# A perceiver layer on one core: order of context tiles, rounded rows and outputs in the cross-attention loop

## The reference

```python
def _L0_xattn_ref(latents, context, cos, sin, ...):
    lat = layer_norm(latents, ln_lat_g, ln_lat_b)          # 16 x 64 x 256
    ctx = layer_norm(context, ln_ctx_g, ln_ctx_b)          # 16 x 1024 x 256
    q = (lat @ Wq)                                         # 16 heads of 64
    k, v = jnp.split(ctx @ Wkv, 2, axis=-1)
    k = apply_rope(k, cos, sin)
    attn = jnp.clip(einsum(q, k) * scale, -11.0, 11.0)
    attn = softmax(attn)
    return (attn @ v) @ Wo + bo
...
x = x + _L0_xattn_ref(_layernorm(x), ctx_1024, ...)
x = x + _L0_attn_ref(_layernorm(x), ...)
x = x + _L0_ffn_ref(_layernorm(x), ...)
```

## Time and profile before

| | |
|---|---|
| runs shown | 1312.22, 1312.03, 1308.29 us; median 1312.03 |
| profiled execution | 1311.06 us, of which 1309.3 are the span of the trace |
| TensorE busy | 1247.5 us, 95% |
| VectorE, ScalarE, GpSimd busy | 936.7, 708.2, 700.2 us |
| mean granted clock of TensorE | 0.989 |
| main loop (first scores to the last step's end) | 50.6 to 1029.3 us |

### The profile page before, as it was taken

The page is one execution under the profiler, slowest core; times in us unless marked ns, Lnnn a source line. Parts: engine busy times, 40 slices in busy tenths (PEclk is TensorE's granted clock), DMA queues, the critical chain, the costliest instruction groups (busy, mean ns, idle before and its releaser), DMA issues.

```text
span 1309.3 us, 40536 instructions
## 1 busy us (share of the span) xinstructions
PE 1247.5 (95%) x16508; PEld 1032.8 (79%) x16508; DVE 936.7 (72%) x1924; ACT 708.2 (54%) x1359; POOL 700.2 (53%) x611
## 2 busy tenths in 40 slices
PE   7999999999999999999999999999999999999997
PEld 3777878778787878787778777787878778799997
DVE  5797777767677777676767767776767256668886
ACT  7655655555555655555555555555643324346664
POOL 3566666666656666566666665666644113334333
PEclk9999999999999999999999999999999989999999
DMA  6344444444444444344434444344445181465662
GB/s 227 83 96 101 107 95 99 99 104 95 94 104 101 103 106 114 92 96 99 108 93 97 98 106 97 94 105 100 106 105 135 35 260 35 156 196 184 189 193 74
DMA packets 92305, 149.95 MB, mean 115 GB/s; under 512 B 28940, under 2 KB 64216, under 8 KB 91992
## 3 DMA queue, kind: packets, MB, share of 16 engines
q1 hardware_dynamic: 88040, 143.13, 42.5%
q0 software_dynamic: 4080, 4.22, 1.6%
HBM read 66.20 MB, written 14.83 MB: 62 GB/s over the span
## 4 chain that ended last, share of the span: by engine, by line
PE 76%; DMA 11%; ACT 4%; DVE 4%; issue 3%; POOL 1%; SPq 1%; POOLq 0%; ACTq 0%; DVEq 0%
PE bank L1424 27%; PE bank L1454 26%; PE bank L1410 9%; DMA out_dram<-ys,result_no 8%; PE bank L1479 3%; PE bank L1434 2%; PE bank L1589 2%; ACT ctf L725 1%; DMA ksw<-kw 1%; PE bank L1618 1%; POOL kr L573 1%; PE bank L1761 1%; PE bank L1661 1%; ACT ct L730 1%; DVE ct L1013 1%
## 5 line engine op out<-in xcount | busy, mean ns | idle before, releaser
L573 POOL TENSOR_TENSOR kr<-kr,ksw 128x1024 f32<-128x1024 f32 x128 | 309.0, 2414 | 351.4 <-DVE pr L973 263.5
L1424 PE MATMUL bank<-ct,wk_hi 128*128 128x512 f32 x1024 | 333.8, 407 | 11.9 <-DVE ct L1013 11.9
L1454 PE MATMUL bank<-p_hi,xc 128*128 128x512 f32 x1024 | 319.5, 393 | 0.0
L725 ACT ACTIVATE ctf<-bank,vecs 128x128 f32<-128x128 f32 x256 | 103.3, 453 | 299.4 <-PE bank L1434 299.4
L1424 PEld LDWEIGHTS bank<-ct,wk_hi 128*128 128x128 f32 x1024 | 184.7, 190 | 54.6 <-issue 13.5
L1454 PEld LDWEIGHTS bank<-p_hi,xc 128*128 128x128 f32 x1024 | 189.6, 188 | 40.2
L1424 PE MATMUL bank<-ct,wk_lo 128*128 128x512 f32 x512 | 202.2, 395 | 0.0
L1454 PE MATMUL bank<-p_lo,xc 128*128 128x512 f32 x512 | 200.7, 392 | 0.0
L1013 DVE TENSOR_TENSOR ct<-ctf,ct 128x256 fp32r<-128x256 f32 x128 | 58.4, 456 | 197.6 <-ACT ct L730 197.5
L1005 DVE TENSOR_TENSOR kw<-bank,stab 128x512 f32<-128x512 f32 x256 | 175.6, 686 | 15.9 <-PE bank L1424 14.8
L996 DVE TENSOR_TENSOR p_lo<-pr,p_hi 128x1024 fp32r<-128x1024 f32 x128 | 184.8, 1444 | 2.2 <-PE bank L1454 1.1
(11 more groups left out here) (215 smaller groups left out, 1740.4 us busy)
## 6 DMA issues: line engine op xcount, KB each, us to landing
ksw<-kw SPq DMA_DIRECT2D x512, 128.0 KB
raw<-in_ctx_dram SPq DMA_DIRECT2D x32, 512.0 KB, 5.2
w_two<-in_L_ffn_W_dram SPq DMA_DIRECT2D x15, 1024.0 KB
x_slots<-fill SPq DMA_DIRECT2D x128, 64.5 KB, 3.0
w_all<-in_L_ffn_W_dram SPq DMA_DIRECT2D x4, 2048.0 KB, 16.8
wo<-in_L_ffn_W_dram SPq DMA_DIRECT2D x7, 1024.0 KB, 5.1
lsum<-l_rows SPq DMA_DIRECT2D x64, 64.0 KB, 2.8
xs<-x_slots SPq DMA_DIRECT2D x23, 129.0 KB, 2.0
```

What stands on the lines that cost most here:

```text
L573: pool.tensor_tensor(kr[:, i], kr[:, i], ksw[:, i], ALU.add).then_inc(kr_done, 1)
L725: last = act.activation(ctf[:, k], psT[:, k * P:(k + 1) * P], ACT.Identity, bias=vecs[:, 3, k:k + 1], scale=vecs[:, 2, k:k + 1])
L1424: last = pe.matmul(psK[:, a * 512:(a + 1) * 512], l[:, k, w], ct[:, h % 3, r, k], start=(m == 0), stop=(m == len(parts) - 1))
L1454: last = pe.matmul(psZ[c], xc[:, slot_, l, t, cols], r[:, i, :, t], start=(f == 0 and m == 0), stop=(f == 1 and m == len(parts) - 1), skip ...
```

## The change

Four things are moved; no arithmetic changes.

- TensorE turns tile j + 9 in step j in place of j + 8, and all that prepares or follows that tile moves with it: its statistics (j + 11), shift and normalisation (j + 10), copies (j + 9). The lead-in begins at step -10, and step -3 is a call of its own before the first keys. The turn waits for `ctf` to be written and not for the rounded part.
- ScalarE writes rounded rows of tile j + 4 in place of j + 5, and POOL their low part.
- TensorE runs outputs directly behind scores, ahead of keys. ScalarE's copy L719 stands ahead of its rounding L707, VectorE's sum L979 ahead of L996. The outputs wait for `ctf` of the tile turned in the step before.
- SP loads context by pairs of tiles, 256 KB, in every even step, each pair with a semaphore of its own.

```diff
-            def context(b, f):
-                i = b % 2 * 2 + f
-                sp.dma_start(raw[:, b % 2, f * HT:(f + 1) * HT], ctx_rows(b, f)).then_inc(ctx_ld[i], 16)
+            def context(b, i):
+                tiles = slice(2 * i, 2 * i + 2)
+                sp.dma_start(raw[:, b % 2, tiles], ctx_1024[b].rearrange("(p t) d -> p t d", t=ST)[:, tiles]).then_inc(ctx_ld[i], 16)
...
-                if j >= 0 and j % 4 == 0 and j // PAIRS + 2 < B:
-                    n, f = j // PAIRS, j % PAIRS // 4
-                    done = n * ST + (f + 1) * HT
-                    sp.wait_ge(xT_ps, done)
-                    sp.wait_ge(x_lo_done, done)
-                    context(n + 2, f)
+                if j >= 0 and j % 2 == 0 and j // PAIRS + 2 < B:
+                    sp.wait_ge(xT_ps, j + 2)
+                    sp.wait_ge(x_lo_done, j + 2)
+                    context(j // PAIRS + 2, j % PAIRS // 2)
...
-                if there(j + 5):
-                    n, t = tile_at(j + 5)
-                    pool.wait_ge(x_hi_done, j + 6)
+                if there(j + 4):
+                    n, t = tile_at(j + 4)
+                    pool.wait_ge(x_hi_done, j + 5)
...
-            for j in range(-5, STEPS):
+            for j in range(-4, STEPS):
                 step(j)
...
-                if there(j):
-                    act.wait_ge(clamp_done, j + 1)
-                    wait(act, z_ps, j // 2 * 2 - 2)
-                    act.copy(step_part(p_hi, j), pr[:]).then_inc(p_hi_done, 1)
-                if there(j + 5):
-                    n, t = tile_at(j + 5)
-                    act.wait_ge(xhat_done, j + 6)
-                    if t == 0 and j + 5 >= 3 * HT:
-                        h = (j + 5) // HT - 3
-                        act.wait_ge(z_ps, h // 2 * PAIRS + h % 2 * 2 + 6)
-                    act.copy(xc[:, n, 0, t, 0:D - 1], raw[:, (j + 5) // ST % 2, (j + 5) % ST, 0:D - 1]).then_inc(x_hi_done, 1)
                 if due(j, 7):
                     n = (j - 7) // 4
                     act.wait_ge(o_ps, n + 1)
                     wait(act, o_done, n)
                     act.copy(o_part[:], psO[1]).then_inc(o_half, 1)
-                if there(j + 8):
+                if there(j):
+                    act.wait_ge(clamp_done, j + 1)
+                    wait(act, z_ps, j // 2 * 2 - 2)
+                    act.copy(step_part(p_hi, j), pr[:]).then_inc(p_hi_done, 1)
+                if there(j + 4):
+                    n, t = tile_at(j + 4)
+                    act.wait_ge(xhat_done, j + 5)
+                    if t == 0 and j + 4 >= 3 * HT:
+                        h = (j + 4) // HT - 3
+                        act.wait_ge(z_ps, h // 2 * PAIRS + h % 2 * 2 + 6)
+                    act.copy(xc[:, n, 0, t, 0:D - 1], raw[:, (j + 4) // ST % 2, (j + 4) % ST, 0:D - 1]).then_inc(x_hi_done, 1)
+                if there(j + 9):
...
                 if g >= 1:
-                    step(g - 9)
+                    step(g - 10)
                 if 0 <= g - 3:
                     latents_high(g - 3)
+            step(-3)
...
                 keys_turned(j, 1)
+                outputs(j)
                 weights_low(j)
-                outputs(j)
                 divided(j)
...
             def turn_context(j):
                 if there(j):
                     pe.wait_ge(xhat_done, j + 1)
-                    wait(pe, ct_hi_done, j)
-                    if due(j - 8, 7):
-                        pe.wait_ge(o_sum, (j - 15) // 4 * 2 + 1)
+                    wait(pe, ctf_done, j)
+                    if due(j - 9, 7):
+                        pe.wait_ge(o_sum, (j - 16) // 4 * 2 + 1)
...
-                    if j + 7 < TILES:
-                        pe.wait_ge(ct_hi_done, j + 8)
+                    if j + 8 < TILES:
+                        pe.wait_ge(ctf_done, j + 9)
...
             def step(j):
                 scores(j)
+                outputs(j)
                 keys(j + 2)
-                outputs(j)
                 sums(j - 2)
                 if j in (STEPS - 2, STEPS - 1):
                     project_heads(j - STEPS + 2, 0, PAIRS)
-                turn_context(j + 8)
+                turn_context(j + 9)
```

More of the change, by code:

```diff
@@ L382, in _ @@
             sp.dma_start(wq_raw[:], Wq.rearrange("(k p) n -> p k n", p=P)).then_inc(wq_ld, 16)
-            context(0, 0)
-            context(0, 1)
+            for i in range(ST // 2):
+                context(0, i)
             sp.dma_start(wk_raw[:], kv[:, :, 0:INNER]).then_inc(wk_ld, 16)
@@ L389, in _ @@
             sp.wait_ge(latT_ps, TT)
-            context(1, 0)
-            context(1, 1)
+            for i in range(ST // 2):
+                context(1, i)
             sp.wait_ge(fill_done, 2)
@@ L686, in step @@
                     act.activation(pr_by_head, heads_by_tile, ACT.Exp, scale=SCALE).then_inc(exp_done, 1)
[L687 to L691, removed]
+                if there(j + 10) and j + 10 >= ST:
+                    i = (j + 10) % 2
+                    x_ = raw[:, (j + 10) // ST % 2, (j + 10) % ST]
+                    act.wait_ge(shift_done, j + 11 - ST)
+                    if j + 10 == ST:
                         act.wait_ge(xhat_done, ST)
@@ L947, in shifts @@
             def shifts(j):
-                if ST <= j + 9 and there(j + 9):
-                    i = (j + 9) % 2
-                    dve.wait_ge(rstd_done, j + 10)
-                    if j + 9 >= ST + 2:
-                        dve.wait_ge(xhat_done, j + 8)
+                if ST <= j + 10 and there(j + 10):
+                    i = (j + 10) % 2
+                    dve.wait_ge(rstd_done, j + 11)
+                    if j + 10 >= ST + 2:
+                        dve.wait_ge(xhat_done, j + 9)
                     dve.scalar_tensor_tensor(out=shift[:, i:i + 1], in0=mv[:, i, 0:1], scalar=-1.0, in1=rstd[:, i:i + 1],
@@ L956, in counted @@
             def counted(j):
-                if ST <= j + 10 and there(j + 10):
-                    n = j + 10
+                if ST <= j + 11 and there(j + 11):
+                    n = j + 11
                     b, t = n // ST, n % ST
-                    if t % HT == 0:
-                        dve.wait_ge(ctx_ld[b % 2 * 2 + t // HT], 16 * (b // 2 + 1))
+                    if t % 2 == 0:
+                        dve.wait_ge(ctx_ld[t // 2], 16 * (b + 1))
                     dve.bn_stats(bst[:, n % 2], raw[:, b % 2, t]).then_inc(bn_done, 1)
             def moments_taken(j):
-                if ST <= j + 10 and there(j + 10):
-                    i = j % 2
-                    dve.wait_ge(bn_done, j + 11)
+                if ST <= j + 11 and there(j + 11):
+                    i = (j + 11) % 2
+                    dve.wait_ge(bn_done, j + 12)
                     dve.bn_aggr(mv[:, i], bst[:, i]).then_inc(stats_done, 1)
@@ L1043, in latents_low @@
                                   ALU.subtract).then_inc(part_lo_done, 1)
-            step(-9)
+            step(-10)
             key_weights(0)
             key_weights(1)
-            for j in range(-8, -2):
+            for j in range(-9, -2):
                 step(j)
-                if j >= -6:
-                    latents_low(j + 6)
+                if -7 <= j <= -4:
+                    latents_low(j + 7)
             query_weights_low(0)
```

37 lines of the change are left out of this document (18 added, 19 removed).

## The result

The kernel after takes 1256.38 us (median of four runs, 1255.76 to 1258.44), the kernel before 1312.05 beside it (four runs, 1308.29 to 1312.22). The ratio is 0.9585, with a 95% interval from 0.9564 to 0.9606. The forecast was 1262 us; it was right in direction and inside its range, and 5.6 us too high. The profiled execution took 1255.76 us around a span of 1254.0.

A forecast was written before the change was run, and what follows sets the result against it. TensorE, busy 95%, was taken to bound the kernel, with gaps from two waits per batch. 23.2 + 12.8 + 8.4 + 4.3 + 2.6 - 1.9 = 49.4 us off 1311.06 gave 1262 us, range 1254 to 1284.

The forecast's parts named there:

- What bounds the kernel: TensorE, busy 95% of 1309.3 us; its gaps are waits of 1.4 us before turns and 0.8 us before keys, fifteen each.
- A: Rounded rows written a step later: ScalarE's 4.1 us wait and the turn's wait go, 1.55 us fifteen times, 23.2 us gained.
- C: Outputs placed next to scores, both 64x64 products: 0.28 us each for 30 outputs, 8.4 us gained, bounds 11.7 and 0.
- B: Tiles turned a step sooner, so keys of a new half do not wait: 0.86 us fifteen times, 12.8 us gained.
- D: Three stretches at a lower granted clock behind the pairs of waits disappear: 4.3 us gained, bounds 0 and 4.3.
- E: Context loaded by pairs, 256 KB: three waits of scores for late additions go, 2.6 us gained, bounds 2.6 and a 2.6 loss.
- slower rival: Swaps in output steps start later, so additions are late and scores wait: thirty steps lose 1.9 us, 1319 us; chance 0.06.
- F: At the start, the loop begins one step earlier with a further turn: a loss of 1.9 us, bounds 0 and 4.
- The wait in a new place: Rival: each of 30 output steps keeps a wait of about 0.6 us, 18 us together, so 1280 us; chance 0.13.
- The clock: Rival: TensorE's clock falls at each group of scores and outputs, 30 times 1.45 us, giving 1305 us; chance 0.05.
- the write of rows was only the last of several: Rival: the turn still waits on other late things, 1274 us, or 1287 if the wait moves one step on; chance 0.06.

The follow-up runs named there:

- experiment 1: Kernel before with only the rounded and low rows written a step later (tile j + 4 in place of j + 5): 1280.91 us, ratio 0.9773.
- experiment 5: Kernel after with rounded rows put back to tile j + 5, everything else as after: 1258.78 us, ratio 0.9592.
- experiment 6: Kernel before with only outputs moved directly behind scores, ScalarE's copy and VectorE's sum put ahead: 1278.36 us, ratio 0.9752.
- experiment 2: Kernel before with only tiles turned a step sooner, their preparation moved along, and one wait added: 1293.88 us, ratio 0.9873.
- experiment 3: Kernel after with outputs back between keys and sums, ScalarE's and VectorE's shares also back, and one wait added: 1263.67 us, ratio 0.9633.
- experiment 7: Kernel after with the turn ahead of sums in the step before an output step: 1255.85 us, ratio 0.9568.
- experiment 4: Kernel after with context loads of four tiles (512 KB) again in place of pairs: 1262.62 us, ratio 0.9634.
- hold_w2: Kernel after with loads of the second expert weights held back until the last outputs are divided: 1255.76 us, ratio 0.9576.
- after_again: Kernel after, unchanged, run once more: 1258.78 us, ratio 0.9607.
- best: Kernel after with the turn ahead of sums before output steps, and VectorE's value-weights work split over steps 2 and 3: 1253.88 us, ratio 0.9564.
- before_again: Kernel before, unchanged, run once more: 1310.04 us in its one run.
- hold_w2_before: Kernel before with loads of the second expert weights held back until the last outputs are divided: 1308.28 us, ratio 0.9972.
- outputs_alone: The same run as experiment 6: kernel before with only outputs moved directly behind scores, 1278.36 us, ratio 0.9752.
- outputs_undone: The same run as experiment 3: kernel after with outputs back between keys and sums, 1263.67 us, ratio 0.9633.

## Why the prediction was right, and where it was not

**What bounds the kernel.** Right. TensorE's gaps were the two events of a batch: with the clock falls behind them they make 40.3 of the 49.96 us that the loop lost, for 51.3 in my sum (its 49.4 without the loss at the start).

**A, 23.2 us.** The size is right, and experiment 1 shows that the rows' move does it alone. The step that failed is the sentence that ScalarE stands ahead of its write, and only then come its half of the outputs, VectorE's sum and the turn. It is true of the kernel before. In the changed kernel that order is gone, since C moves the half of the outputs to the front. I listed that move under C and priced it only by what it delays, not by what it frees. Experiments 5 and 6 show that in the full change A is worth nothing measurable and C carries the 23.2. The sum held because I counted them once.

**B, 12.8 us.** Right, by experiment 2; nothing became late next. (0.86 x 15 is 12.9.) Steps 32 and the like are 6.99.

**C, 8.4 us.** Measured 6.6 in step lengths and 6.9 by experiment 3. The start of the outputs came out at +1.03, for +1.04 predicted, and the slack ahead of the turn at 0.68 us, for 0.7. What was mis-sized is the outputs' own length: I took the whole of step 127's 0.94 for scores and outputs side by side and added 0.11 of wait, which makes 1.05; it is 1.10. The 0.1 us of wait is real: experiment 7 takes it away.

**D, 4.3 us.** Right. I had only three falls behind fifteen pairs of waits, and took all of it; experiments 1, 2 and 6 show that in the loop it takes the pair.

**E, 2.6 us.** The three late additions are gone, 2.7 us, and the fourteen profiles counted under experiment 4 bear out that pairs end them. Their size is partly luck: with the rest of the change in place, loads of four tiles cost only 0.6 us in the one profile of it, another profile of the kernel before loses 1.2, and experiment 1 has none of them with loads of 512 KB. The landing time was mis-sized: a pair takes 4.0 us, for 3.1 interpolated, and 5.2 for four tiles. By an estimate from the fit of the Trainium skill (DMA: Bandwidth & Descriptors, "Anatomy of one DMA"), made for transfers that GpSimd issues, the pair would land 0.6 us sooner than four tiles. The trace has 1.2, and my interpolation had 2.1. POOL's wait for swaps, which my slower rival feared, is 118.2 us in 35 waits, for 76.6 in 27 before, but the same loop has 77.2 in 27 in hold_w2: the pairs did not bring it. TensorE's scores waited for the addition once, 1.5 us at the end of step 4.

**F, a loss of 1.9 us.** 0.94 in the first pair of profiles, 1.9 in the second. The start of one and the same kernel varies by 0.8 (before) and 1.8 us (after), and the longer start of each has more time at the lower level of the clock. The nine starts without any such time are 50.6 to 51.2 us with the old order of turns and 51.6 to 52.0 with the new. So the added step costs about 0.9 us, and my 1.9 was twice that.

**What the sum lacked.** The tail, 6.3 and 4.4 us in two pairs of profiles. Most of it is the clock, as the traces account for it; no run changes the clock alone. Behind the loop, and up to the last few microseconds of the span, TensorE's granted clock is at its lower level for 13.7 us in the kernel before and never in the kernel after; half of that is 6.8 us, for the 6.3 measured. The fall goes with TensorE's wait for VectorE at the output projection. In the four profiles where that wait is 0.2 to 1.0 us (after, after_again, hold_w2 and best) no fall goes with it, and the tails are 280.8 to 283.0 us. In the ten where it is 1.6 to 4.0 us the clock falls within the wait or less than 1 us behind it every time, and the tails are 283.9 to 289.2. With half of the time at the lower level taken off, all fourteen tails are 280.8 to 283.5. What stays open is what sets the wait, and why the fall is longest, 10 us for 3 to 7, in the four profiles with the old order of turns and rows (before, before_again, hold_w2_before and outputs_alone), though two of their waits, 1.8 and 2.0 us, are no longer than others. outputs_undone waits 2.0 us there, as the kernel before does, and its clock is at the lower level for a third of the time:

```profile
1007.45 1.79 PE L1588 MATMUL bank<-wo,qo 128*128 128x256 f32 x4 [2.00 <-DVE raw L1072]
```

```profile
1007.00:1017.00 10.00, 9.55 (x102) 8.00 (x104) 3.78 (x10) 2.33 (x7) 1.43 (x3) 0.83 1.09 354
```

Start and loop by themselves give 1311.06 - 49.0 = 1262.0, for the sum's 1261.7. That this is so close is in part luck: C was 1.8 us too high and step 4 took 0.6, while F's loss was 1.0 too high and the loop's small change brought 1.0.

**The rivals.** None came true. The wait in a new place exists, at 0.1 us instead of 0.6. Scores did not wait for the addition more often. The clock stayed at 1.00 through thirty groups of quarter-array products. That the write of rows was only the last of several fell with experiment 1.

## What to carry to other kernels

Where several parts of a change cut the same chain, price the chain once, and ask of each part alone what it would leave: here two of four parts were each enough for 23 of the 50 us. Look for waits that recur with one length and one period before looking at work, and where two follow close on each other look whether the granted clock falls behind them, here and there only, as it did in 10 of 45 cases here. Small groups of products with a small tile go beside others of that kind, and the copy they wait for is best made a whole group earlier.

## What the runs showed that I had not expected

A granted clock of about 0.8 follows the two waits of 1.4 and 0.8 us in only ten of 45 cases, six of them at the two steps that fell in all three profiles, and costs 1.3 to 1.6 us each time; in the loop a single wait of either length never brought it. Fourteen tails of the same work differ by 8 us, and by less than 3 once the time at the lower level of the clock is taken out. And 64 products of 64x64 have three prices, 1.33, 1.10 and 0.95 us, by their neighbours and by a 0.1 us wait in front of them.
